# Feed-forward stage: tokens in natural order, a strided read moved to the pool engine, one wait and the loads moved

## The reference

```python
def _L0_ffn_ref(x, gamma_x, gamma_slot, slot_embeds, w1, w2):
    xn = rms_norm(x, gamma_x)
    se = rms_norm(slot_embeds, gamma_slot)
    logits = jnp.einsum('bsd,etd->bset', xn, se)
    dispatch = jax.nn.softmax(logits, axis=1)              # over the tokens
    slots = jnp.einsum('bsd,bset->betd', xn, dispatch)
    h = jax.nn.gelu(slots @ w1, approximate=False)
    processed = h @ w2
    combine = jax.nn.softmax(logits.reshape(b, s, e * t), axis=-1)   # over the slots
    return jnp.einsum('bnd,bsn->bsd', processed.reshape(b, e * t, d), combine)

x = _layernorm(x + _L0_attn_ref(x, wq, wk, wv, wo))
x = _layernorm(x + _L0_ffn_ref(x, ...))
```

## Time and profile before

| what | value |
|---|---|
| three timed runs | 1880.22, 1880.42, 1883.98 us; median 1880.42 |
| the profiled execution's own time | 1878.56 us |
| its span in the profile | 1876.5 us, 2.06 us less than its own time |
| TensorE's mean granted clock | 0.977 of full speed |
| TensorE busy | 1769.6 us, 94% of the span |
| DVE, ACT, POOL busy | 77%, 66%, 59% |

### The profile page before, as it was taken

How to read it: one execution, slowest core, us unless ns; L and a number is a source line. 1 busy time by engine, 2 the same in 40 slices (tenths; PEclk the granted TensorE clock), 3 DMA queues, 4 the chain that set the end, 5 groups by cost and what they waited for, 6 DMA issues and landing times. The chain is left out here.

```text
span 1876.5 us, 33405 instructions
## 1 busy us (share of the span) xinstructions
PE 1769.6 (94%) x10524; PEld 1549.9 (83%) x10524; DVE 1445.8 (77%) x2947; ACT 1238.9 (66%) x2362; POOL 1114.7 (59%) x696
## 2 busy tenths in 40 slices
PE   4999999999999999999999999999999469999997
PEld 4788888887888888888888888888888458889987
DVE  3889888987898889879978898888889455565543
ACT  2777777776777777777777777777777235444442
POOL 3666666665666566656665666666665244555544
PEclk7999999999999999999999999999999789999999
DMA  3322322232223222322232233222222211222211
GB/s 102 84 76 77 79 80 68 68 81 80 69 80 95 81 75 68 91 69 68 69 95 70 80 84 92 69 68 68 80 73 74 85 40 40 52 51 58 60 28 34
DMA packets 76679, 134.24 MB, mean 72 GB/s; under 512 B 19296, under 2 KB 45920, under 8 KB 76512
## 3 DMA queue, kind: packets, MB, share of 16 engines
q1 hardware_dynamic: 75328, 131.15, 26.5%
q10 hardware_dynamic: 1184, 1.05, 0.2%
HBM read 56.36 MB, written 8.70 MB: 35 GB/s over the span
## 5 line engine op out<-in xcount | busy, mean ns | idle before, releaser
L454 ACT ACTIVATE probs<-ps_slot,neg_max 128x640 f32<-128x640 f32 (+7 forms) x512 | 379.1, 742 | 124.0 <-DVE neg_max L540 114.6
L540 DVE CUSTOM_DVE_ANT_0 ps_slot<-ps_slot,causal 128x640 f32<-128x640 f32 (+7 forms) x512 | 387.1, 756 | 49.1 <-PE ps_slot L57 47.3
L691 PE MATMUL ps_turn<-ident,probs 128*128 128x128 f32 x2304 | 340.8, 277 | 18.0 <-DVE x_t L597 5.9
L691 PEld LDWEIGHTS ps_turn<-ident,probs 128*128 128x128 f32 x2304 | 256.9, 141 | 52.8 <-DVE x_t L597 7.6
L418 POOL TENSOR_TENSOR q<-rot_q,q 128x1024 fp32r<-128x1024 f32 x64 | 153.9, 2405 | 237.9 <-ACT q L471 237.9
L55 PE MATMUL ps_slot<-k,q 128*128 128x512 f32 (+3 forms) x768 | 283.5, 369 | 2.3 <-DVE rot_q L556 1.4
L56 PE MATMUL ps_slot<-k,q 128*128 128x512 f32 (+3 forms) x768 | 266.4, 347 | 0.0
L57 PE MATMUL ps_slot<-k,q 128*128 128x512 f32 (+3 forms) x768 | 266.0, 346 | 0.0
L410 POOL TENSOR_TENSOR swapped_q<-swapped_q,rope 128x1024 f32<-128x1024 f32 x64 | 163.9, 2561 | 77.9 <-DMA swapped_q<-unrot_q 77.8
L418 POOL TENSOR_TENSOR k<-rot_k,k 128x1024 fp32r<-128x1024 f32 x64 | 153.3, 2395 | 87.5 <-ACT k L471 86.4
L410 POOL TENSOR_TENSOR swapped_k<-swapped_k,rope 128x1024 f32<-128x1024 f32 x64 | 153.7, 2401 | 55.6 <-DMA swapped_k<-unrot_k 55.5
(11 more groups left out here) (159 smaller groups left out, 4527.4 us busy)
## 6 DMA issues: line engine op xcount, KB each, us to landing
swapped_k<-unrot_k SPq DMA_DIRECT2D x128, 256.0 KB, 3.6
swapped_q<-unrot_q SPq DMA_DIRECT2D x128, 256.0 KB, 3.6
inv_b<-inv_rows SPq DMA_DIRECT2D x64, 512.0 KB, 4.8
x_rows<-in_L_attn_x SPq DMA_DIRECT2D x8, 512.0 KB, 5.0
y_t<-y_sum SPq DMA_DIRECT2D x8, 512.0 KB, 5.2
row_b<-r_rows SPq DMA_DIRECT2D x16, 256.0 KB, 4.1
y_in<-y_t SPq DMA_DIRECT2D x7, 512.0 KB, 6.1
x_row<-in_L_attn_x SPq DMA_DIRECT2D x7, 512.0 KB, 7.3
```

The costliest lines, as they stand in the source:

```text
L454: act.activation(probs_tile(t), score_tile(name, head, i), ACT.Exp, scale=-1.0, bias=neg_max[:, head.par, t:t + 1], accum_out=sums[:, head ...
L540: dve.tensor_tensor_reduce(tile, tile, causal[:, T - WIDTH[t]:T], -1.0, UNSEEN, ALU.add, ALU.min, neg_max[:, head.par, t:t + 1]).then_inc( ...
L691: last = pe.transpose(bank[:, at:at + P], probs_tile(t)[:, j * P:(j + 1) * P], ident[:, :])
```

## The change

- The interleaving is dropped for `z_t` and all that follows from it: `split_zt` copies straight, and `turn_tile` and `sum_out` read 128 adjacent columns. `token_transposes` keeps its step, as `y_t` is still interleaved.
- The row maxima still arrive interleaved in `row_b`. POOL's `sub_rows` reads them with the step of 16 bytes. They are positive now (`row_peak`) and are subtracted.
- `peak_b` holds the negated slot maxima. SP stores `neg_peak` as soon as `find_peak` is done and doesn't wait for `peak`. `find_row_peak` subtracts and takes the maximum. On DVE `turn_peaks` stands behind `copy_proc`.
- SP issues the two loads only after `peak_b` has landed.
- `input_rows` is cut in halves. Each stands ahead of the `sub_rows` of its half, and waits only for that half's `add2`.
- TensorE waits for `zt_lo` ahead of `turn_slots`, behind `sum_out(2)`, and no longer ahead of `sum_out(2)`.

```diff
--- before
+++ after
         peak = s.sb("peak", [P, 2, NC], F32)
-        neg_row = s.sb("neg_row", [P, 2, NT], F32)
+        row_peak = s.sb("row_peak", [P, 2, NT], F32)
         inv_slot = s.sb("inv_slot", [P, NC], F32)
...
-        def by_token(cols, t):
-
-            return cols.rearrange("q (p t) -> q t p", t=4)[:, t % 4, :]
+        def token_cols(t):
+            return slice(t * P, (t + 1) * P)
...
             def spread_peaks(b, par, first):
-                wait_apart(sp, peak_made, b + 1, sp_ticks)
-                sp.dma_start(c_rows[par, :].rearrange("(p c) -> p c", c=NC), peak[:, par, :])\
+                wait_apart(sp, peaked, b * NC + NC, sp_ticks)
+                sp.dma_start(c_rows[par, :].rearrange("(p c) -> p c", c=NC), neg_peak[:, par, :])\
                   .then_inc(peak_stored, 16)
...
             def spread_rows(b, par, half, first):
...
                 own = r_rows[par:par + 1, half_cols(half)]
-                sp.dma_start(own.rearrange("a (p t) -> p (a t)", t=4), neg_row[:, par, half_tiles(half)])\
+                sp.dma_start(own.rearrange("a (p t) -> p (a t)", t=4), row_peak[:, par, half_tiles(half)])\
                   .then_inc(row_stored[half], 16)
...
                     wait_apart(sp, added1, b * 2 + 2, sp_ticks)
+                    wait_apart(sp, peak_landed, b * 16 + 16, sp_ticks)
                     load(b + 2)
...
-            def input_rows(b, par, first):
-                if not first:
-                    wait_apart(pool, added2, b * 4 - 4, ticks)
-                for t in range(NT):
+            def input_rows(b, par, half, first):
+                if not first:
+                    wait_apart(pool, added2, b * 4 - 4 - 2 * (1 - half), ticks)
+                for t in range(NT // 2 * half, NT // 2 * (half + 1)):
                     last = pool.tensor_scalar(x1[par][:, t, :], res[:, t, :], neg_mean[:, 0, t:t + 1],
...
                 for c in range(NC):
-                    pool.tensor_tensor(comb[:, c, half_cols(half)], logits[par][:, c, half_cols(half)],
-                                       row_b[:, half, :], ALU.add).then_inc(subbed, 1)
+                    out, src = (rows.rearrange("q (t p) -> q t p", t=4) for rows in
+                                (comb[:, c, half_cols(half)], logits[par][:, c, half_cols(half)]))
+                    pool.tensor_tensor(out, src, row_b[:, half, :].rearrange("q (p t) -> q t p", t=4),
+                                       ALU.subtract).then_inc(subbed, 1)
...
                 first_norm(0, first_normed, half_tiles(half))
-            input_rows(0, 0, True)
+            for half in range(2):
+                input_rows(0, 0, half, True)
...
                 for half in range(2):
+                    if ahead:
+                        input_rows(b + 1, 1 - par, half, first)
                     sub_rows(b, par, half, first)
-                if ahead:
-                    input_rows(b + 1, 1 - par, first)
                 if not first:
...
             def split_zt(half, made, value, src, done):
                 act.wait_ge(made, value)
-                act.activation(z_t[:, 0, half_cols(half)].rearrange("d (p t) -> d p t", t=4),
-                               src.rearrange("d (t p) -> d p t", t=4), ACT.Copy).then_inc(done, 1)
+                act.activation(z_t[:, 0, half_cols(half)], src, ACT.Copy).then_inc(done, 1)
...
             def add1(b, half):
                 dve.wait_ge(in_landed, b * 32)
-                dve.wait_ge(x1_made, b)
+                dve.wait_ge(x1_made, b * 2)
                 dve.wait_ge(tokens_turned, b * 2 - (1 - half))
...
             def split_zt(half, made, value, src, done):
                 dve.wait_ge(made, value)
-                out = z_t[:, :, half_cols(half)].rearrange("d a (p t) -> d a p t", t=4)
-                dve.tensor_tensor(out[:, 1, :, :], src.rearrange("d (t p) -> d p t", t=4), f32(out[:, 0, :, :]),
+                dve.tensor_tensor(z_t[:, 1, half_cols(half)], src, f32(z_t[:, 0, half_cols(half)]),
                                   ALU.subtract).then_inc(done, 1)
...
                 tile = tile_bank(t).rearrange("q (c p) -> q p c", c=NC)
-                dve.tensor_tensor_reduce(tile, tile, peak_b[:, :].rearrange("q (p c) -> q p c", c=NC), -1.0, UNSEEN,
-                                         ALU.add, ALU.min, neg_row[:, par, t:t + 1]).then_inc(row_peaked, 1)
+                dve.tensor_tensor_reduce(tile, tile, peak_b[:, :].rearrange("q (p c) -> q p c", c=NC), 1.0, -UNSEEN,
+                                         ALU.subtract, ALU.max, row_peak[:, par, t:t + 1]).then_inc(row_peaked, 1)
...
             def add2(b, par, q):
                 dve.wait_ge(out_summed, b * 4 + (q + 1))
-                dve.wait_ge(x1_made, b + 1)
+                dve.wait_ge(x1_made, b * 2 + (q // 2 + 1))
                 dve.wait_ge(out_made, b * NT + 1)
...
             def batch(b, par, first, ahead):
...
                     find_peak(b, par, c)
+                if not first:
+                    copy_proc(b - 1)
                 turn_peaks(b, par)
-                if not first:
-                    copy_proc(b - 1)
                 if ahead:
...
+            def y_tokens(half, t):
+                return y_in[:, half_cols(half)].rearrange("d (p t) -> d t p", t=4)[:, t, :]
+
             def token_transposes(half, bank, done):
                 for t in range(4):
-                    last = pe.transpose(bank[:, t * P:(t + 1) * P], by_token(y_in[:, half_cols(half)], t), ident[:, :])
+                    last = pe.transpose(bank[:, t * P:(t + 1) * P], y_tokens(half, t), ident[:, :])
                 last.then_inc(done, 1)
...
                     last = pe.transpose(tile_bank(t)[:, c * P:(c + 1) * P],
-                                        by_token(logits[par][:, c, half_cols(t // 4)], t), ident[:, :])
+                                        logits[par][:, c, token_cols(t)], ident[:, :])
                 last.then_inc(tile_turned, 1)
...
                         last = pe.matmul(out_bank(q)[:, i * D1:(i + 1) * D1],
-                                         by_token(comb[:, c, half_cols(q // 2)], t), proc[:, c, :],
+                                         comb[:, c, token_cols(t)], proc[:, c, :],
                                          start=c == 0, stop=c == NC - 1)
...
                     z_transposes(1 - par, 1, turn("z1"), z_turned)
-                    pe.wait_ge(zt_lo, b * 2 + 1)
                 if not first:
...
                     sum_out(2)
+                if ahead:
+                    pe.wait_ge(zt_lo, b * 2 + 1)
                 turn_slots(b)
```

More of the change, by code:

```diff
@@ L1267, in batch @@
                     find_peak(b, par, c)
-                turn_peaks(b, par)
                 if not first:
                     copy_proc(b - 1)
+                turn_peaks(b, par)
                 if ahead:
```

## The result

The changed kernel takes 1808.39 us (median of four runs, 1805.92 to 1808.98), where four runs of the kernel before on the same chip had a median of 1880.78. The ratio is 0.9609, with a 95% interval of 0.9593 to 0.9626. The forecast was 1807.0. The profiled execution took 1805.92 us with a span of 1803.9, so the spans differ by 72.6 us where the sum said 73.4.

What follows compares the result with a forecast made beforehand. TensorE, busy 94% of the span, was taken to bound the kernel. Gains of 61.9, 2.6, 2.0, 7.0 and 1.3 made 74.8 us, less 1.4; 1880.42 less 73.4 gave 1807, range 1798 to 1812 (0.70).

Steps and rivals of the forecast that it cites:

- Stationary operand of `sum_out`: TensorE's `sum_out` without the step: pitch falls from 233 to 112 ns over 512 instructions, 61.9 us gained.
- The fourth rival: The step is not what slows `sum_out`; the 61.9 us is gone, about 1871 us; chance 0.04.
- `turn_tile` 2.6: TensorE's transposes without the step: 10 ns each, 0.3 us a turn, 2.6 us gained over 8 batches.
- `turn_slots` 2.0: TensorE's 4 transposes between two strided calls take 0.86 us for 0.45; 0.4 gained in 5 turns, 2.0 us.
- The wait for `zt_lo`, 7.0: TensorE's 1.16 us idle ahead of `sum_out(2)` goes in six turns: 7.0 us gained.
- The 0.1 us that was to come back: Ahead of `find_hidden`, `slot_in` needs 2.31 us with 2.23 of cover: a 0.1 us stall a turn, 7 turns.
- `peak_b`, 1.3 us in the first batch: Landing some 1.9 us earlier, it shortens TensorE's 3.73 us first-batch stall: 1.3 us gained.
- The third rival: Late `peak_b` delays the tile sweep 1 us in six turns, 1813 us; chance 0.20 shared with POOL's rival.
- The unknown s: Length of one strided POOL `sub_rows`: 1.24 to 1.28 us without step; allowed up to 1.91, 1.49 if maxima are late.
- the quick case: Row maxima come as quickly as today, so POOL's `sub_rows(0)` starts at 1615.4 and one instruction may last 1.91 us.
- the rival's mechanism: POOL's step becomes the bound: its chain is late in five turns, 1818 to 1835 us; chance 0.20 shared with `peak_b`.
- The end: The last batch's 64 `sum_out` instructions lie on the path and gain too, less 0.4 us for POOL's queued norm.

Runs made afterwards that it cites:

- E1: The changed kernel with the 16-byte step put back in the stationary operand of `sum_out` alone: 1868.44 us.
- E2: The kernel before with only the stationary operand of `sum_out` read without a step: 1822.38 us.
- E7: The changed kernel with the 16-byte step back in `turn_tile`'s stationary operand alone: 1814.25 us.
- E3: The changed kernel with the wait for `zt_lo` back ahead of `sum_out(2)`: 1815.89 us.
- the ten kernels above: Ten kernels that wait for `peak_b` and keep the first batch's sweep order: 46.8 to 49.0 us from first `find_logits` to first `sum_out(0)`.
- E4: The changed kernel with the two loads issued right behind `peak_b`, without waiting for its landing: 1810.39 us.
- E6: The changed kernel with all three operands of POOL's `sub_rows` at a step of 16 bytes: 1818.65 us.
- E11: The changed kernel with four more `sub_rows` on POOL in each turn, written to a spare tile: 1830.41 us.
- E5: The changed kernel with `row_b` read without a step in POOL's `sub_rows`: 1807.42 us.
- E12: The changed kernel with `sum_slots(1)` behind `turn_tile(2)`, and the last batch's `add2` waiting only for its own output rows: 1807.23 us.
- E13: The changed kernel with `sum_slots(1)` behind `turn_tile(2)` in batches 1 to 7, earlier last `add2`, last-but-one store halved, POOL's norm before its wait: 1801.43 us.
- E8: The changed kernel with a step of 8 bytes in `sum_out`'s stationary operand: 1813.47 us in its one run.

## Why the prediction was right

**Stationary operand of `sum_out`, 61.9 us.** Right in cause and size. E1 and E2 put 60 us on this one operand from either side. The fourth rival fell with that. Within the turns E1 loses 283.40 - 230.08 = 53.3 us of it.

**`turn_tile` 2.6, `turn_slots` 2.0.** E7 lost 2.2 us in the turns, and the sweep of the first batch comes on top. The second was misread. I took the 0.86 us of the earlier trace rows for the price of standing between two strided calls, in five turns. Timeline of PE in the first turn of the kernel before, then in one of E1, which has the step in `sum_out` too:

```profile
1581.45 0.60 PE L1360 MATMUL ps_turn<-ident,slot_row 128*128 128x128 f32 x4
1581.89 3.89 PE L1383 MATMUL ps_slot<-proc,comb 128*128 128x129 f32 x16
```

```profile
1622.45 0.60 PE L1364 MATMUL ps_turn<-ident,slot_row 128*128 128x128 f32 x4
1622.89 3.89 PE L1387 MATMUL ps_slot<-proc,comb 128*128 128x129 f32 x16
```

Both take 0.44 us between strided calls, as four of the seven turns before and all seven of E1 do. Only in the three turns of 43.85 us is it 0.86, and a window of it shows the clock:

```profile
1624.96:1625.82 0.86, 0.86 (x6) 0.86 (x5) 0.58 (x3) 0.00 (x0) 0.00 (x0) 0.50 0.00 0
```

So these were 3 x 0.42 = 1.3 us of the lower of the clock's levels, not 2.0 of a step. TensorE had idled for 1.16 us and worked through `sum_out(2)` before; three of the other turns did the same and kept the full clock. None of the kernels with only the wait or only the step shows it (E1, E2, E3), each in one profile; what brings it is open.

**The wait for `zt_lo`, 7.0.** E3's brackets give 7.0 us and its turns 1.4 each, 8.6 in six. The 0.1 us that was to come back ahead of `find_hidden` did not show. With this the turns add up: 53.3 of the operand, 8.6 of the wait, 2.2 of `turn_tile` and 1.3 of the clock are 65.4 of the 65.5 us.

**`peak_b`, 1.3 us in the first batch.** The stall shrank by more, from 3.73 to 1.59 us, but the stretch by only 0.7. That is inside the scatter of the ten kernels above (46.8 to 49.0 us), so the difference of these two can't be told from nothing. By its parts: up to `turn_tile(2)` 16.64 us for 19.26, from there to `find_hidden` 14.76 for 14.30, from there to `sum_out(0)` 16.71 for 15.27. PE's timeline, after, in the last part:

```profile
1539.32 0.63 PE L57 MATMUL ps_slot<-slot_in,w_s 128*128 128x512 f32 x1
...
1542.49 0.40 PE L56 MATMUL ps_slot<-slot_in,w_s 128*128 128x512 f32 x1
```

Until 1542 the records of 512 columns last 0.63 us and start 0.43 apart, after that 0.39 to 0.40 and 0.23 apart, as they do in the kernel before from the start of this part. So the clock has first the lower of its levels (1.2 GHz), then the upper (2.4 GHz). The granted clock is 0.50 from 1538.90 to 1541.88; in the kernel before it is 1.00 from 1539.79 to 1545.00, behind stalls of the same length (1.17 and 1.66 us after, 1.16 and 1.66 before). So in this execution a part of what the shorter stall gave was lost to the lower clock, and what brought it on is open.

**The third rival** (1 us a turn for late maxima) did not come. It had them used 6.2 us after their issue. Even with the loads issued at once, E4 used them after 4.87 us and E2 after 5.32, and what stands behind took 2.8 us for the 3.1 I counted; in E2 that was just in time.

**POOL.** The unknown s came out at 1.55 us in the records, 1.51 in pitch. `sub_rows(0)` started 13.9 to 14.8 us into the turns, at or ahead of the early end of the forecast's 14.6 to 18.0, so the quick case held. The spare 3.0 us is 0.38 an instruction over eight: the threshold in the tightest turn was 1.51 + 0.38 = 1.89, and the quick case had said 1.91. E6 shows that the rival's mechanism, DVE waiting for `z_scale`, is real behind it; E11 does not show it. Its price was too high, though. In E6 four instructions take 8.41 us, 2.10 each; by the rival's sum that is 8 x (2.10 - 1.89) = 1.7 us late in a turn and 8.4 in five. By the spare time of each of the five turns it is 5.5. They lost 3.2, of which 1.6 came this way. In E6 `z_scale` is done 9.8 to 10.4 us into the turn, where `scale_rows` starts at 9.7 in the kernel after: at most 0.7 late. A turn that has grown gives POOL's chain that much more time up to the next one, which the rival's sum left out; how much of the rest this explains was not tried. And the sum had no term for what E11 shows, a `turn_peaks` on DVE that lasts until POOL's `sub_rows` are over. The GPSIMD Engine Reference of the Trainium skill, "Performance pitfalls for Q7 kernels", places the cost at steps over 8 bytes, and the runs agree: 1299 ns at 8 bytes, 1553 at 16, 1281 without. Its size they don't bear out for one stepped operand of three: +21%, not about +50%. With all three stepped it is +67%.

**The end, the term that was mis-sized.** I gave the end its share of `sum_out`, 64 x 121 ns = 7.7 us, less 0.4, and it gave 5.0. The sums did shrink, from 15.20 to 7.41 us, but they no longer set the end. Timelines of DVE and POOL, after:

```profile
1790.70 0.17 DVE L1227 RECIPROCAL inv_out<-ps_slot 128x2 f32<-128x2 f32 x1 [5.43 <-POOL out_row L1027]
```

```profile
1787.12 3.45 POOL L1027 TENSOR_SCALAR out_row<-res,neg_mean,rstd 128x128 f32<-128x128 f32 x8 [0.31 <-POOL rstd L1010]
1794.15 0.20 POOL L1008 TENSOR_SCALAR neg_mean<-mv 128x4 f32<-128x4 f32 x1 [3.58 <-DMA out<-out_row]
```

POOL's chain, its 8 `sub_rows`, a norm, the output rows of batch 6, and then the landing of their store ends last. The step on POOL has about 1 us of this (in E5 DVE's wait is 4.28 us), E12 shows that DVE's start costs nothing, and E13 that the landing and what stands around it cost 2. By stretches the sum had 64.5 us for the turns, 1.6 for the first batch and 7.3 for the end; measured were 65.5, 0.7 and 5.0, and 1.4 of scatter ahead of them. So the misses of +1.0, -0.9, -2.3 and +1.4 nearly cancel: 72.6 for 73.4. The total was closer than its parts.

## What to carry to other kernels

Where weight loads set TensorE's pace, look at the step of the stationary operand: here float32 columns 16 bytes apart cost some 120 ns an instruction, and 8 bytes apart some 5. A step that must be somewhere can go to an engine with slack; work out that slack in the turn as it will be, and name the start that it hangs on. Read more than one turn for it: here one turn in five had 3.0 us where the others had 3.7 or more, and one place that looked like the price of a step was the clock of three turns. Then lay out the first and the last batch by themselves: what bounds the turns need not bound them, and here the end was worth 2 us more once its own chain was read.

## What the runs showed of the hardware

- TensorE's pitch and its load don't follow each other one to one. In `turn_tile` the load grew from 142 to 208 ns and the pitch by 10 ns; in `sum_out` the load grew from 191 to 328 ns and the pitch by 121. At 8 bytes (E8) its load is 196 ns and its pitch 118 for 112.
- On POOL the cost of steps adds up over the operands: 1281, 1553 and 2142 ns for none, one and three at 16 bytes.
- The 256 KB of `peak_b` landed in 3.6 us in the median with the loads held back, in 4.7 with them issued 1.4 us behind it (E4), and with them 1.1 us behind it in 5.1 (E2) and 5.8 (before). So the distance alone does not set it; what else does was not tried.
- A copy of 128x4 on DVE (`turn_peaks`) that takes 0.16 to 0.28 us in the kernel after took 1.9 to 2.2 us in E11, and ended with POOL's last `sub_rows`, within 0.1 us, in all six turns. In E6 it took 0.3 to 1.0 us in four turns, again ending with POOL's. No run moved only one of the two.
- With the same code ahead, the first `find_logits` starts up to 4.6 us apart between executions. A difference of 2 us is read from the turns, not from spans. The lower clock falls at other places of the first batch in each of them.
